# Thirteen pairs for a live expert tile, ten for the last four, and weight loads handed out two slots at a time

## Time and profile before

| | |
|---|---|
| median of 3 runs | 1441.13 us (1440.92 to 1446.17) |
| the profiled execution | 1447.18 us, span 1445.4 us |
| granted TensorE clock, mean | 0.910 |
| PE busy | 1269.6 us (88%) |
| DVE busy | 1195.8 us (83%) |
| POOL busy | 1115.1 us (77%) |
| ACT busy | 755.0 us (52%) |

### The profile page before, as it was taken

How to read it: one execution, slowest core, us unless ns; L and a number is a source line. 1 busy time by engine, 2 the same in 40 slices (tenths; PEclk the granted TensorE clock), 3 DMA queues, 4 the chain that set the end, 5 groups by cost and what they waited for, 6 DMA issues and landing times.

```text
span 1445.4 us, 21600 instructions
## 1 busy us (share of the span) xinstructions
PE 1269.6 (88%) x5800; PEld 922.5 (64%) x5800; DVE 1195.8 (83%) x1618; ACT 755.0 (52%) x1613; POOL 1115.1 (77%) x1090
## 2 busy tenths in 40 slices
PE   5847799999989999999999997999999999787530
PEld 5735367777667777777777775777777777444110
DVE  6747479998769888988889886988899889999968
ACT  1352466555645566555655564555655575655311
POOL 0356279797879789888999787888998798998653
PEclk9978899999989999999999999999999999555555
DMA  7111265446344635654474454464465345475447
GB/s 211 50 37 51 59 208 167 130 158 183 120 136 134 211 120 160 204 151 120 151 227 129 147 183 134 139 202 130 145 201 170 116 144 161 143 233 167 139 133 231
DMA packets 124963, 218.02 MB, mean 151 GB/s; under 512 B 15264, under 2 KB 40992, under 8 KB 124832
## 3 DMA queue, kind: packets, MB, share of 16 engines
q10 hardware_dynamic: 73728, 134.25, 31.8%
q1 hardware_dynamic: 43616, 61.82, 13.2%
q0 software_dynamic: 7488, 20.46, 4.3%
HBM read 191.57 MB, written 24.90 MB: 150 GB/s over the span
## 4 chain that ended last, share of the span: by engine, by line
PE 73%; DVE 8%; POOL 7%; issue 4%; ACT 4%; DMA 3%; SPq 1%; ACTq 0%; DVEq 0%; POOLq 0%
PE bank L1175 31%; PE bank L1144 16%; PE bank L1122 8%; PE bank L1188 7%; POOL arena L405 3%; DVE arena L940 3%; PE bank L1051 2%; PE bank L1087 1%; PE bank L1013 1%; PE bank L1067 1%; PE bank L1060 1%; DMA arena<-delta_d 1%; PE bank L1020 1%; DVE arena L1003 1%; DVE arena L999 1%
## 5 line engine op out<-in xcount | busy, mean ns | idle before, releaser
L405 POOL TENSOR_TENSOR arena<-arena,c_rep 128x512 f32<-128x512 f32 x512 | 602.7, 1182 | 160.4 <-DVE arena L940 146.8
L940 DVE TENSOR_TENSOR_SCAN arena<-bank,carry,arena 128x512 f32<-128x512 f32 x512 | 652.7, 1275 | 35.7 <-ACT bank L711 34.0
L1175 PE MATMUL bank<-xgT,wring 128*128 128x256 f32 x2240 | 541.3, 385 | 17.7 <-SPq L321 15.4
L1175 PEld LDWEIGHTS bank<-xgT,wring 128*128 128x128 f32 x2240 | 421.4, 191 | 141.0 <-issue 81.5
L711 ACT ACTIVATE bank<-arena,a_neg 128x512 f32<-128x512 f32 x512 | 354.4, 692 | 101.6 <-DVE arena L940 47.5
L931 DVE TENSOR_TENSOR arena<-bank,b_rep 128x512 f32<-128x512 f32 x512 | 351.6, 687 | 58.7 <-PE bank L1188 42.3
L1188 PE MATMUL bank<-stack,pick 128*128 128x512 f32 x512 | 312.9, 612 | 36.1 <-DVE arena L931 36.0
L635 ACT ACTIVATE th<-bank 128x256 f32<-128x256 f32 x312 | 119.4, 383 | 321.4 <-PE bank L1175 288.1
L1144 PE MATMUL bank<-wring,hid 128*128 128x256 f32 x1120 | 268.6, 382 | 0.3 <-POOL hid L420 0.2
L1144 PEld LDWEIGHTS bank<-wring,hid 128*128 128x128 f32 x1120 | 209.5, 190 | 59.4 <-issue 27.7
L420 POOL TENSOR_TENSOR hid<-gt,ue 128x256 f32<-128x256 f32 x312 | 227.5, 729 | 13.7 <-DVE gt L952 13.0
(11 more groups left out here) (167 smaller groups left out, 868.4 us busy)
## 6 DMA issues: line engine op xcount, KB each, us to landing
arena<-delta_d ACTq DMA_DIRECT2D x512, 256.0 KB
wring<-in_w_all SPq DMA_DIRECT2D x64, 384.0 KB, 5.1
arena<-results SPq DMA_DIRECT2D x16, 512.0 KB, 6.4
xn<-in_x SPq DMA_DIRECT2D x4, 1024.0 KB, 9.7
xn_d<-xn SPq DMA_DIRECT2D x4, 1024.0 KB, 5.9
parts_d<-spare SPq DMA_DIRECT2D x16, 256.0 KB, 2.8
stack<-parts_d SPq DMA_DIRECT2D x16, 256.0 KB
out<-arena SPq DMA_DIRECT2D x8, 512.0 KB, 3.2
```

The lines of the kernel that those rows point to most:

```text
L405: pool.tensor_tensor(p_ring[:, s % P_RING, :], h_ring[:, s % H_RING, :], of_chunk(c_rep, c, 2), ALU.mult).then_inc(s_hc, 1)
L940: v.tensor_tensor_scan(out=h_ring[:, s % H_RING, :], data0=a_bank[s % 2][:, :], data1=b_ring[:, s % B_RING, :], initial=carry[:, q:q + 1], ...
L1175: ins = pe.matmul(bank[:, m * SLOT:(m + 1) * SLOT], wring[:, kk, (2 * m + h) * P:(2 * m + h + 1) * P], xgT[:, i % 2, h, :], start=(h == 0) ...
```

## The change

A tile is given 13 pairs if its number is below 35, and 10 if it is one of the last four. In a tile of 13, steps stand where they did, outs 6 and 7 move from pair 14 to pair 15, and pair 12 is marked as empty. In a tile of 10, step k stands at pair k, the outs at 3, 5, 7 and 9, the next rows at 4. The last out is then at pair 510 instead of 486. `next_free` takes a marked pair if one lies within five pairs of the wanted one, else the first free one as before. On SP `load_weights` now gets a list of slots: it is called at the pair of each two outs of tile i for the same two slots of tile i + 1, ahead of where the whole call stood, and branches each time. ACT and POOL get a call each for the outs of the last pairs.

```diff
-TILE_PAIRS = 12
+LONG_TILES = 35
+LONG, SHORT = 13, 10
...
     for i in range(TILES):
-        first = MOE_FIRST + TILE_PAIRS * i
+        first = MOE_FIRST + LONG * min(i, LONG_TILES) + SHORT * max(i - LONG_TILES, 0)
+        spare = [first + 12] if i < LONG_TILES else []
         for k in range(KS):
-            by_pair[first + 3 * (k // 2) + k % 2].append(("step", i, k))
-            by_pair[first + 3 * (k // 2) + 5].append(("out", i, k))
+            if i < LONG_TILES:
+                step, out = first + 3 * (k // 2) + k % 2, first + 3 * (k // 2) + (5 if k < 6 else 6)
+            else:
+                step, out = first + k, first + 2 * (k // 2) + 3
+            by_pair[step].append(("step", i, k))
+            by_pair[out].append(("out", i, k))
         if i + 1 < TILES:
-            by_pair[first + 8].append(("rows", i + 1, 0))
+            by_pair[first + (8 if i < LONG_TILES else 4)].append(("rows", i + 1, 0))
+        empty.update(spare)
 
     def next_free(s):
 
-        return next(p for p in range(s, PAIR_COUNT) if all(kind == "out" for kind, i, k in by_pair[p]))
+        free = [p for p in range(s, PAIR_COUNT) if all(kind == "out" for kind, i, k in by_pair[p])]
+        return next((p for p in free if p in empty and p < s + 5), free[0])
...
-            def load_weights(i):
-
-                row = sp.value_load(row_i[0:1, i:i + 1], min_val=0, max_val=(E - 1) * KS)
-                new = sp.value_load(new_i[0:1, i:i + 1], min_val=0, max_val=1)
-                with sp.If(new > 0):
-                    for k in range(KS):
+            rows_at, is_new = {}, {}
+
+            def load_weights(i, slots):
+
+                if i not in rows_at:
+                    rows_at[i] = sp.value_load(row_i[0:1, i:i + 1], min_val=0, max_val=(E - 1) * KS)
+                    is_new[i] = sp.value_load(new_i[0:1, i:i + 1], min_val=0, max_val=1)
+                with sp.If(is_new[i] > 0):
+                    for k in slots:
                         ge(sp, s_o, KS * (i - 1) + k + 1)
...
-                    load_weights(0)
-                for turn, i, k in BY_PAIR[s]:
-                    if turn == "step" and k == 0 and i:
-                        load_weights(i)
+                    load_weights(0, range(KS))
+                done = [(i, k) for turn, i, k in BY_PAIR[s] if turn == "out"]
+                if done and done[0][0] + 1 < TILES:
+                    load_weights(done[0][0] + 1, [k for i, k in done])
...
             state_by_c(PAIR_COUNT - 1)
+            for here in BY_PAIR[PAIR_COUNT - 2:PAIR_COUNT]:
+                after_outs(here)
...
                 turns(BY_PAIR[s])
+            outs(BY_PAIR[PAIR_COUNT - 1])
             save_carry(PAIR_COUNT // 4 - 1)
```

More of the change, by code:

```diff
@@ L48, in turns_by_pair @@
 def turns_by_pair():
-    by_pair = [[] for _ in range(PAIR_COUNT + 1)]
+    by_pair, empty = [[] for _ in range(PAIR_COUNT + 1)], set()
     by_pair[MOE_FIRST - 1].append(("rows", 0, 0))
     for i in range(TILES):
-        first = MOE_FIRST + TILE_PAIRS * i
+        first = MOE_FIRST + LONG * min(i, LONG_TILES) + SHORT * max(i - LONG_TILES, 0)
+        spare = [first + 12] if i < LONG_TILES else []
         for k in range(KS):
-            by_pair[first + 3 * (k // 2) + k % 2].append(("step", i, k))
-            by_pair[first + 3 * (k // 2) + 5].append(("out", i, k))
+            if i < LONG_TILES:
[4 more added lines that the diff above has]
+            by_pair[out].append(("out", i, k))
         if i + 1 < TILES:
-            by_pair[first + 8].append(("rows", i + 1, 0))
+            by_pair[first + (8 if i < LONG_TILES else 4)].append(("rows", i + 1, 0))
+        empty.update(spare)
     def next_free(s):
-        return next(p for p in range(s, PAIR_COUNT) if all(kind == "out" for kind, i, k in by_pair[p]))
+        free = [p for p in range(s, PAIR_COUNT) if all(kind == "out" for kind, i, k in by_pair[p])]
+        return next((p for p in free if p in empty and p < s + 5), free[0])
     for c in range(NC):
@@ L307, in load_stack @@
                                  parts_d[n, :, cols(c)].rearrange("(j c) t -> c j t", c=64)).then_inc(s_stack[c % 2], 16)
-            def load_weights(i):
-                row = sp.value_load(row_i[0:1, i:i + 1], min_val=0, max_val=(E - 1) * KS)
-                new = sp.value_load(new_i[0:1, i:i + 1], min_val=0, max_val=1)
-                with sp.If(new > 0):
-                    for k in range(KS):
+            rows_at, is_new = {}, {}
[5 more added lines that the diff above has]
+                    for k in slots:
                         ge(sp, s_o, KS * (i - 1) + k + 1)
-                        sp.dma_start(wring[:, k, :], w_all[bass.ds(row + k, 1), :, :].rearrange("a p c -> p (a c)")
+                        sp.dma_start(wring[:, k, :], w_all[bass.ds(rows_at[i] + k, 1), :, :].rearrange("a p c -> p (a c)")
                                      ).then_inc(s_w[k], 16)
                 with sp.Else():
-                    for k in range(KS):
+                    for k in slots:
                         ge(sp, s_o, KS * (i - 1) + k + 1)
```

## The result

| | before | after |
|---|---|---|
| median | 1441.67 us (4 runs) | 1401.94 us (4 runs, 1398.48 to 1406.96) |
| ratio | | 0.972, interval 0.9685 to 0.9754 |
| the profiled execution | 1447.18 us, span 1445.4 | 1398.48 us, span 1396.4 |

The kernel is 40 us faster. The forecast was 57 us in 1441, 1384 us. 1401.94 lies inside the range of eight in ten, but 2 us above the likeliest case (1372 to 1400), at the lower edge of the bracket that was given to the local limits of DVE and POOL. The four runs lie in two groups, 1398.5 and 1399.3 us at a mean granted clock of 0.93 and 1404.6 and 1407.0 us at 0.91, and the profile is of the fastest.

A forecast was written before the change was run, and what follows sets the result against it. PE's own work was taken to bound the live tiles, POOL's the last four. Pair 471 at 1234 for 1303.4, last multiply -59.6, end +1.9: -57.7, 1389.5 profiled, in proportion 1384 us; eight in ten 1366 to 1412.

The forecast's parts named there:

- the likeliest case: Whole kernel: a time between 1372 and 1400 us, given a chance of 0.60.
- the local limits of DVE and POOL: Whole kernel: 1400 to 1425 us if DVE and POOL hold PE up locally under the live tiles; chance 0.17.
- Three stalls: Pairs 16 to 436: PE's three waits for weights and the slow clock behind two of them go, -21.6 us.
- PE's price of a pair: Live tiles: a further pair costs PE a spread and a quarter of a quad, 0.55 us; 35 pairs +19.1.
- Local losses: Pairs 16 to 471: PE waiting in empty pairs and at POOL's bursts, 8 us for both together.
- The rival of DVE's full time: Live tiles: an empty pair costs DVE's full time, up to 46 us instead of 8, so 1422; bracket's chance 0.17.
- The dead stretch: Pairs 471 to 511, the ten-pair tiles: POOL's summed work sets it, 91 us, where it was 79.99.
- The end: Behind the last multiply: last scatter's issue and landing, 5.1 instead of 3.2 us to the first result transfer, +1.9.
- POOL's lag: Around pair 471: POOL runs about 2 us behind, so its last multiply ends at 1234 + 2 + 91 = 1327.
- sign of being wrong: Wrong if PE waits for `hid` or POOL's multiply over 15 us in all, or weights are late elsewhere.
- Another sign: Last four tiles: POOL busy over 95%, with DVE waiting for it.
- The slower rival: Whole kernel: hand-overs pace each pair at 2.46 us whatever it holds, +25 us, some 1466; chance 0.07.

The follow-up runs named there:

- the first experiment: The kernel before (twelve pairs a tile) with only the new load_weights and its calls by twos: 1423.43 us, ratio 0.9865.
- rows apart: Changed kernel; in ten-pair tiles the rows have pair 4 for themselves, steps at 0 to 3 and 5 to 8, outs at 4, 6, 9, 11 (last tile 10): 1392.53 us.
- late outs: Changed kernel with the outs of the ten-pair tiles one pair later (4, 6, 8, 10): 1395.54 us, ratio 0.9671.

## Why the prediction was right, and where it was off

From pair 16 on the prediction gives -57.7 and the profile -42.0. Step by step:

- *Three stalls, -21.6.* Right within 2.4 us: 19.2 us in the trace of the first experiment, and no wait for weights in the changed kernel. That the plan of pairs alone would take the old stalls away as well I hadn't seen; for the total it makes no difference.
- *PE's price of a pair, 0.55.* Spreads and quads took 358.1 us at twelve pairs (first experiment) and 380.6 at thirteen: 22.5 for 35 pairs, 0.64 each. PE's busy time over the whole stretch went from 1011.4 to 1036.8, 25.4 instead of 19.1, by this price and since the 35 pairs from 436 to 471 also hold a pair of `down` products (2.2 us) and one more start of a chunk (1.3), which I hadn't counted. Thirteen tiles without a product took 27.5 us on average in the first experiment, and ten of them 28.3 in the changed kernel, from 27.0 to 29.5; 28.0 to 28.3 was forecast.
- *Local losses, 8.* PE was idle 1046.97 - 1036.84 = 10.1 us, but 4.0 of it was there at twelve pairs too, so 6.1 is new. The rival of DVE's full time, 46 us, is refuted at thirteen pairs and nearly comes true at fourteen. With the two lines above (2.4 and 6.3 us more, 1.9 less here) the stretch is 1047.0 for 1040: 7 us off.
- *The dead stretch, 91 from POOL's amount.* This is the term that was mis-sized: 98.81, 7.8 us more. I had added up engines and set the slowest. What I left out is the chain of one step: the out stands two pairs behind, POOL has two scatters in between, and PE stops. With the outs a pair later the stretch is 90.2, with rows apart 88.2. The amount itself was well priced. The sum has the last multiply end 2 + 91 = 93 us behind the scan of pair 471; it was 102.8 in the changed kernel, 94.7 with late outs and 93.4 with rows apart. It is only that the amount didn't set the changed kernel.
- *The end, +1.9, and POOL's lag.* After, the last rows were these:

```profile
1333.22 3.69 POOL L416 TENSOR_TENSOR arena<-arena,c_rep 128x512 f32<-128x512 f32 x3
...
1338.40 0.97 POOL L437 DMA_INDIRECT results<-o_sb,dest  x1 [0.30 <-issue]
...
1340.90 6.99 SPq L366 DMA_DIRECT2D arena<-results  x8
```

The last multiply ends 3.95 us behind the scan of pair 511; I had let that lag vanish in POOL's sum, with 2 left: 2 us. From there to the first result transfer it is 3.99 us, where it was 2.78 and not the 3.2 of the prediction: +1.2. Without a scatter behind the last multiply (the run without the dead tiles' gathers and scatters) it is 2.78 again. SP's last wait ahead of it is the one for the scatters, and the transfer starts 1.5 us behind the last scatter's issue; my 2.4 for the landing was too much.

So -57.7 + 7.0 + 7.8 + 2.0 - 0.7 = -41.6, which is the measured -42.0 within 0.4.

The number is inside the range, yet the prediction's own sign of being wrong came true. It named more than 15 us of waits of PE for `hid` or POOL's multiply; the changed kernel has 24.9 for `hid` and 7.2 for the multiply, where they were 1.7 and 6.8. Another sign failed with it: POOL was to be busy over 95% in the last four tiles with DVE waiting for it, and it was busy 85%, with POOL waiting for DVE and PE for POOL. The signs of the live stretch (no wait for weights, clock 1.00, a few us of spread waits) held. So the account of the live stretch was right, and that of the dead stretch had the wrong limit.

The multiply on POOL in chunk 6 and in chunk 7 of the changed kernel (ns min/median/max):

```profile
L416 POOL TENSOR_TENSOR arena<-arena,c_rep x64: 1078/1090/1110, 1037.3 to 1181.5; 128x512 f32<-128x512 f32 x64
L416 POOL TENSOR_TENSOR arena<-arena,c_rep x64: 1250/1272/1294, 1182.9 to 1335.7; 128x512 f32<-128x512 f32 x64
```

The sum's 1.27 us is what all multiplies of the dead stretch take. The two lengths go by chunk: in all eleven profiles of this case the multiply takes 1.08 to 1.13 us in chunks 0, 2, 4 and 6 (but one or two at the very start) and 1.25 to 1.33 in chunks 1, 3, 5 and 7. DVE's scan is 1.27 us in every chunk, and its work beside POOL is the same, so DVE isn't the cause. By the rule of the Trainium skill (SBUF — State Buffer, "SBUF: two separate sides") DVE instructions that read only one input from SBUF don't hold GpSimd up. The trace agrees with that, and the prediction was wrong to say that it doesn't bear the page out: a multiply of 1.08 us in the dead stretch, chunk 7, doesn't follow from the page. What changes with the chunk is the part of `c_rep` that the multiply reads, whose start moves by 514 elements a chunk; that its place is the cause wasn't tried.

The slower rival (a pace of hand-overs) falls for the live stretch, and lives on in small for the dead one: there it was hand-overs, and not work, that cost the last 8.6 us.

Left open: how much of the remaining 4.8 us (88.2 against DVE's 83.4) is POOL's amount and how much order in the version with rows apart, and whether fewer than ten pairs for a dead tile would do better; neither was tried.

## What to carry to other kernels

Laying a free stream of work under a stretch that another engine bounds costs only that engine's share, up to the point where the two engines' sums meet; work that point out in us per period (here the thirteenth pair cost 0.90 us and the fourteenth 1.78). When a period is shortened, adding up engines isn't enough: follow one item round the engines and count how many slots it has, and what else stands in each in-order queue on the way. Experiments on two parts of one change may not add up, because each can remove the same stall.

## What was not expected of the hardware

The start, in which the change has no part, varies by up to 7 us. Pair 16 began at 187.18 us in the profile of the changed kernel and at 192.33 in that of the weight calls alone. The changed kernel from 150 to 187 us:

```profile
150.00:187.00 37.00, 28.32 (x105) 12.85 (x105) 22.12 (x28) 20.34 (x38) 13.49 (x13) 1.00 0.45 148
```

The kernel before with the weight calls alone, in the same window:

```profile
150.00:187.00 37.00, 29.28 (x87) 12.90 (x87) 17.71 (x23) 16.63 (x31) 10.87 (x10) 0.86 0.30 98
```

Up to 150 us both had done the same 416 of PE's products. From there the one with the granted clock at 1.00 throughout has done 105 where the other, at 0.86, has done 87. PE has gaps in both. In the eleven profiles of this case the clock of this window was 0.86 in four, the kernel before among them, with pair 16 at 191.8 to 194.2 us, and 1.00 in seven, with pair 16 at 187.2 to 190.1, though the program is the same up to there. What decides between the two isn't shown. A difference of a few us between two single profiles is thus better read from a mark behind the start, here pair 16.
